# Mamba and local attention, one core: sums over states and the skip term as accumulating DMAs into device memory, in place of pair sums and identity matmuls

## What is computed

```python
dt = softplus(dt_lr @ dt_proj_w.T + dt_proj_b)
dA = exp(einsum('bld,dn->bldn', dt, -exp(A_log)))
dBx = einsum('bld,bln->bldn', dt * x_conv, B_ssm)
h = a_t * h + bx_t                      # scan over tokens
y_t = einsum('bdn,bn->bd', h, c_t)      # sum over 16 states
y = ys + x_conv * D_param               # skip term
out = (y * silu(z)) @ out_proj_w.T
```

## Time and profile before

| what | us |
|---|---|
| median of three runs | 2499.3 |
| profiled execution, its own time | 2501.03 |
| its span, first to last instruction | 2499.2 |
| VectorE (DVE) busy | 2325.9 (93%) |
| TensorE (PE) busy | 2211.9 (89%) |
| ScalarE (ACT) busy | 1336.3 (53%) |
| GpSimd (POOL) busy | 1094.6 (44%) |
| mean granted TensorE clock | 0.957 of full speed |
| DMA | 225.89 MB, mean 90 GB/s |

### The profile page before, as it was taken

How to read it: one execution, slowest core, us unless ns; L and a number is a source line. 1 busy time by engine, 2 the same in 40 slices (tenths; PEclk the granted TensorE clock), 3 DMA queues, 4 the chain that set the end, 5 groups by cost and what they waited for, 6 DMA issues and landing times. The chain is left out here.

```text
span 2499.2 us, 36377 instructions
## 1 busy us (share of the span) xinstructions
PE 2211.9 (89%) x11008; PEld 1363.6 (55%) x11008; DVE 2325.9 (93%) x3159; ACT 1336.3 (53%) x2816; POOL 1094.6 (44%) x973
## 2 busy tenths in 40 slices
PE   4699889998899989989898998989889898899888
PEld 1365555555555555555564655555455555555556
DVE  5999999999999989999899999999999999999984
ACT  3455554555455654546546555465554555555442
POOL 3534355354343553534534436443464425553540
PEclk8899999999999999999999999999999999999999
DMA  3222222222232123222222222322222222222220
GB/s 131 86 91 87 99 81 103 102 73 105 70 124 82 67 102 113 84 97 81 96 87 99 81 95 87 106 85 72 97 101 100 91 74 93 88 98 84 101 85 15
DMA packets 70512, 225.89 MB, mean 90 GB/s; under 512 B 7648, under 2 KB 36640, under 8 KB 51632
## 3 DMA queue, kind: packets, MB, share of 16 engines
q1 hardware_dynamic: 70320, 223.57, 24.8%
HBM read 214.63 MB, written 4.72 MB: 88 GB/s over the span
## 5 line engine op out<-in xcount | busy, mean ns | idle before, releaser
L604 DVE TENSOR_TENSOR_SCAN hb<-dA,state,hb 128x512 f32<-128x512 f32 x512 | 688.5, 1345 | 13.8 <-ACT dA L853 5.6
L1014 POOL COPY state<-hb 128x2 f32<-128x2 f32 x256 | 220.0, 862 | 919.8 <-DVE hb L604 919.8
L1267 PE MATMUL ring<-hT,w 128*128 128x256 f32 (+1 forms) x1536 | 378.4, 405 | 26.7 <-ACT hT L956 26.7
L853 ACT ACTIVATE dA<-dt_sb,amat 128x512 f32<-128x512 f32 x512 | 345.1, 717 | 101.7 <-PE ysum L1131 66.6
L597 DVE TENSOR_TENSOR hb<-u_sb,bc 128x1024 f32<-128x1024 f32 x256 | 350.6, 1370 | 19.9 <-POOL state L1014 19.9
L1267 PEld LDWEIGHTS ring<-hT,w 128*128 128x128 f32 (+1 forms) x1536 | 288.0, 192 | 122.1 <-ACT hT L956 33.8
L611 DVE TENSOR_TENSOR dA<-hb,bc 128x1024 f32<-128x1024 f32 x256 | 327.3, 1279 | 0.0
L935 ACT ACTIVATE probs<-ring,nmax 128x256 f32<-128x256 f32 x512 | 235.3, 476 | 142.3 <-DVE nmax L726 142.2
L1131 PE MATMUL ysum<-dA,ident 128*128 128x512 f32 x512 | 264.1, 611 | 2.8 <-DVE dA L618 2.7
L1060 POOL TENSOR_TENSOR rnorm<-rnorm,powers 128x8 f32<-128x8 f32 x128 | 248.2, 1939 | 23.7 <-POOL rnorm L1057 21.2
L618 DVE TENSOR_TENSOR dA<-dA 128x512 f32<-128x512 f32 x256 | 222.4, 869 | 0.0
(11 more groups left out here) (109 smaller groups left out, 3569.0 us busy)
## 6 DMA issues: line engine op xcount, KB each, us to landing
bc<-bc_rows SPq DMA_DIRECT2D x128, 1024.0 KB, 4.7
wqkv<-in_wqkv SPq DMA_DIRECT2D x48, 512.0 KB, 6.1
w<-in_w SPq DMA_DIRECT2D x16, 1364.0 KB, 8.3
w<-in_w SPq DMA_DIRECT2D x16, 768.0 KB, 5.2
tab<-in_tab SPq DMA_DIRECT2D x64, 128.0 KB, 4.5
xtok<-in_x SPq DMA_DIRECT2D x16, 256.0 KB, 2.9
xres<-in_x SPq DMA_DIRECT2D x16, 256.0 KB, 5.3
out_y<-X SPq DMA_DIRECT2D x16, 256.0 KB, 3.4
```

The lines of the kernel that those rows point to most:

```text
L604: dve.tensor_tensor_scan(hb[:, k % H_RING, :], dA[:, k % DA_RING, :], hb[:, k % H_RING, :], state[:, k:k + 1], ALU.mult, ALU.add).then_inc ...
L853: act.activation(dA[:, k % DA_RING, :], dt_sb[:, j, :], ACT.Exp, scale=amat[:, n:n + 1]).then_inc(dA_ready.sem, 1)
L1014: pool.tensor_copy(state[:, 2 * m:2 * m + 2], hb[:, slot:slot + 2, T - 1]).then_inc(state_saved.sem, 1)
L1267: m = pe.matmul(bank(it, ("h", f, i))[0:rows, part * 256:(part + 1) * 256], w1[:, ft, col:col + rows], hT[:, ft, :], start=(ft == 0), stop ...
```

## The change

The sum of the pairs, the sum over groups and the skip term leave VectorE, TensorE and PSUM. For each pair, GpSimd issues one DMA of both hC tiles (128 partitions x 1024 elements, 512 KB) to a buffer `ysum[j]` in device memory: the first of a half overwrites, the seven others of the tile add to it there (`accum_op=ALU.add`). ScalarE scales xconv by D in place (stage `skip`), and GpSimd adds it with another DMA of 256 KB. At the end of a half GpSimd adds the second 512 columns of `ysum[j]` to the first (stage `merge`, device memory to device memory), SP loads the result into a new tile `y_sb` (stage `y`), and the gate reads that in place of PSUM. Every adding DMA waits, in GpSimd's queue, for the landing of the one before it on the same j. A dA tile is free when the DMA of its pair has landed. The ring of PSUM banks grows from five to seven. The weights `wo` are kept for one layer and loaded per layer (stage `wol`, 512 KB). All five orders are written anew. The scratch of GpSimd's DMAs doubles.

```diff
-BANKS = 5
+BANKS = 7
+ADDS = STATES // GROUP + 2
...
-    diag = sb("diag", [P, NJ, P])
-    ybank = [ctx.enter_context(nc.psum_tensor(f"ysum{j}", [P, T], f32)) for j in range(JH)]
+    ysum = nc.dram_tensor("ysum", [NJ, P, GROUP * T], f32, kind="Internal").ap()
+    y_sb = sb("y_sb", [P, JH, T])
...
+            def load_y(half):
+                for jj in range(JH):
+                    j = half * JH + jj
+                    sp.wait_ge(*added[j].at(it, D16 * ADDS))
+                    sp.wait_ge(*gated.at(it, (half - 1) * JH + jj + 1))
+                    sp.dma_start(y_sb[:, jj, :], ysum[j, :, 0:T]).then_inc(y_loaded[j].sem, D16)
...
-                    dve.wait_ge(*summed.at(it, (half + 1) * SUMS // HALVES - JH + jj + 1))
-                    dve.tensor_tensor(sz[:, j, :], ybank[jj][:, :], sz[:, j, :], ALU.mult)
+                    dve.wait_ge(*y_loaded[j].at(it, D16))
+                    dve.tensor_tensor(sz[:, j, :], y_sb[:, jj, :], sz[:, j, :], ALU.mult)
...
-                if at_ring:
-                    act.wait_ge(*summed.at(it, m + 1))
-                else:
-                    act.wait_ge(*pair_added.at(it, m + 1))
+                if before >= 0:
+                    gb, jb, _ = unit(kb)
+                    act.wait_ge(*added[jb].at(before, adds_after(gb)))
...
+            def add_to_y(m):
+                g, j, _ = unit(2 * m)
+                first = g % (NGROUPS // HALVES) == 0
+                out = 2 * m % DA_RING
+                pool.wait_ge(*hC_ready.at(it, m + 1))
+                if first:
+                    pool.wait_ge(*y_loaded[j].at(it - 1, D16))
+                else:
+                    pool.wait_ge(*added[j].at(it, adds_after(g) - D16))
+                pool.dma_start(ysum[j, :, :], dA[:, out:out + 2, :].rearrange("p n t -> p (n t)"),
+                               accum_op=ALU.bypass if first else ALU.add).then_inc(added[j].sem, D16)
+            def add_skip(half):
+                for j in range(half * JH, half * JH + JH):
+                    pool.wait_ge(*added[j].at(it, D16))
+                    pool.wait_ge(*skip_ready.at(it, j + 1))
+                    pool.dma_start(ysum[j, :, 0:T], xconv[:, j, :], accum_op=ALU.add)
+            def add_halves(half):
+                for j in range(half * JH, half * JH + JH):
+                    pool.wait_ge(*added[j].at(it, D16 * (ADDS - 1)))
+                    pool.dma_start(ysum[j, :, 0:T], ysum[j, :, T:2 * T], accum_op=ALU.add)
...
+            def load_wo(l):
+                sp.wait_ge(*filled(it if l else it - 1, ("wo", NW - 1 if l else NA - 1)))
+                sp.dma_start(wo[:, :, :], io["wo"][:, l, :, :]).then_inc(wo_loaded.sem, D16)
```

More of the change, by code:

```diff
@@ L82 @@
[L82 to L86, removed]
+o(7,2) o(7,3) wo(7) +heads(0) +s(0,0) +s(0,1) +dt(2) +v(0) +pT(0,0) +q(1) hT(3) +dt(3) h(3,0) h(3,1) h(3,2)
@@ L92 @@
[L92 to L96, removed]
@@ L124 @@
-+scan +q(5) ++tail +turn(q,5) +turn(k,5) +scan +scan +q(6) +scan +scan +scan +stats(2) +turn(q,6) +scan
-+turn(k,6) +scan +q(7) ++q(0) +turn(q,7) +turn(k,7) +scan +scan +carry2 +scan
+add(30) +turn(q,0) scan +turn(k,0) add(31) +q(1) +scan +add(0) stats(3) merge(1) +scan +add(1) +scan
++skip(0) ++halo +scan +scan +add(2) +add(3) +turn(q,1) +q(2) +scan +turn(k,1) +scan +add(4) +add(5)
++turn(q,2) +scan +add(6) +add(7) +turn(k,2) +scan +scan ++norm(0) +add(8) +add(9) +q(3) +stats(0) +scan
++turn(q,3) +turn(k,3) +scan +add(10) +add(11) +add(12) +scan +scan +scan ++norm(1) +q(4) +add(13) +carry
@@ L126 @@
++scan +scan +add(14) +add(15) +turn(q,4) +turn(k,4) +add(16) +scan +add(17) +stats(1) +merge(0) +scan
++skip(1) +scan +scan +q(5) +add(18) +add(19) +turn(q,5) +turn(k,5) +scan +add(20) +add(21) +scan +add(22)
++add(23) +scan +scan +q(6) +turn(q,6) +turn(k,6) +q(7) +scan +add(24) +add(25) +scan +stats(2) +turn(q,7)
++turn(k,7) +scan +scan +add(26) +add(27) +add(28) +scan +add(29) +carry2 ++q(0) ++tail +scan
 """
 SP_ORDER = """
-+bc(1) wo(7) +bc(2) xres(1) +bc(3) +q(1) +w1(0) store(0) ++x(0) store(1) +bc(4) +k(1) +k(2) ++x(1) +bc(5)
@@ L577, in _ @@
         dve.tensor_copy(identb[:, :], ident[:, :]).then_inc(casts_done, 1)
-        for j in range(NJ):
-            dve.tensor_scalar(diag[:, j, :], ident[:, :], par[:, C_DP + j:C_DP + j + 1], None, ALU.mult)\
-               .then_inc(diag_ready, 1)
         dve.wait_ge(casts_done, 3)
@@ L624, in fill @@
                 if at_unit[0] == CHUNKS * UNITS:
-                    for _ in range(3):
+                    for _ in range(2):
                         step()
@@ L1100, in stages @@
             return {"halo": load_halo, "norm": rstd_of_x, "tail": save_halo, "q": scale_tables,
-                    "turn": scale_heads, "stats": rstd_of, "scan": keep_state, "carry": carry_xn,
+                    "turn": scale_heads, "stats": rstd_of, "scan": keep_state, "add": add_to_y, "skip": add_skip, "merge": add_halves, "carry": carry_xn,
                     "carry2": carry_x2}
```

178 lines of the change are left out of this document (92 added, 86 removed).

## The result

The kernel became slower: 2533.8 us (median of four runs, 2530.3 to 2539.0) against 2499.5 measured beside it on the same chip, a ratio of 1.014 [1.012, 1.016]. The forecast was 2350, and the range ended at 2480.

What follows compares the result with a forecast made beforehand. VectorE's own work, busy 93% of the span, was taken to set the pace. 2501 - 175 - 25 + 20 + 10 + 15 + 5 = 2351, said as 2350 us; range 2270 to 2480.

Steps and rivals of the forecast that it cites:

- Pair sums off VectorE: VectorE's 256 pair sums leave: 148 us saved if all waiting inside them moves over, 200 if none; with small parts -175.
- Matmuls off TensorE and banks: 297 us off TensorE worth nothing by itself; with two further banks VectorE's waits shorten, bounds 0 and -60, taken -25.
- DMAs on GpSimd: 320 issues at 1 us in GpSimd's queue, covered except ahead of state copies: +20, bounds 0 and +130.
- dA tiles held by a DMA: A dA tile is free only when its add lands, taken 5 us: +10 on today's 5.6 us wait, bounds 0 and +50.
- Load on the DMA engines: DMA share rises from 25% to about 45, at most 65%; shifted rows land later, 32 waits by 0.5 us: +15.
- Scaling on ScalarE: 32 more passes at 0.6 us, 19 us on an engine idle for 47% of the span: zero.
- The way of y: Last add, merge, SP's load and second gate, about 10 us behind some 15 us of VectorE work: +5, bounds 0 and +40.
- Everything hidden: Rival: all waiting goes along with the pair sums and the new order finds 25 us: 2275; 12%.
- GpSimd's queue: Rival: at 2.5 us per issue GpSimd becomes the second bound, 128 us lost at state copies: 2460; 15%.
- Issues and VectorE lock each other out: Rival: each issue holds VectorE's next instruction, 0.5 us giving 2510, 0.2 us giving 2415; 13%.
- Adding DMAs saturate: Rival: over 6.5 us of all sixteen engines per add makes DMA the bound; at 8 us 2930; 13%.
- I would be wrong outright if VectorE waited mostly for something that has no line today: Sign of outright failure: VectorE waiting mostly for something without a line in the earlier waits, y or the B and C rows.

Runs made afterwards that it cites:

- late k weights: Kernel after, with SP loading the next chunk's k weights right after q(7) instead of behind wo(6): 2461.8 us, 72 us less than the kernel after.
- 256 small adds: Kernel before, its own sum untouched, with 256 adding DMAs of 64 KB issued by GpSimd beside it to buffers nobody reads: 2534.8 us.
- plain writes: Kernel before with 256 DMAs of 512 KB writing beside it: 2543.4 us. Kernel after, sum's DMAs writing instead of adding: 2452.1 us, with k weights loaded earlier 2402.0.
- full adds: Kernel before, its own sum untouched, with 256 adding DMAs of 512 KB issued by GpSimd beside it to buffers nobody reads: 2599.6 us.
- the late load alone: Kernel before with only SP's order changed, the next chunk's k weights and two table loads moved behind the shift: 2524.3 us, +24 us.
- six-bank kernel: Kernel after with the k weights loaded earlier and six instead of seven PSUM banks in the ring: 2588.7 us, 127 us more than with seven.
- the small adds: Kernel after with k weights loaded earlier and the seven later adds of each half and tile cut to 128 of 1024 columns: 2395.2 us.

## Why the prediction was wrong, step by step

Two terms of the sum failed, the pair sums (-175, measured -78) and the load on the DMA engines (+15, measured +56 to +67), and one cause had no term at all, the late k weights (+72). The effects measured in separate kernels make this account, and they need not add up exactly: pair sums -78, 256 small adds +35, from small adds to plain writes +9, from these to the full adds +56, late k weights +72. From 2499.5 that gives 2593.5; the kernel after took 2533.8. The rest, -60, is everything that these kernels don't single out: the new order with its banks, the skip term and the merges, the way of y, and what the effects do to each other (the late load alone costs 24, 50 or 72 us, by its surroundings). With plain writes and the early load it comes out alike: 2500 - 78 + 35 + 9 = 2466 against 2402.0, -64.

*Pair sums off VectorE, -175: failed, measured -78.* The busy time came out at the forecast's 2151 us both without the pair sums and in the kernel after (2151.2). That it fits to the microsecond is luck, since 174 was the middle of 148 and 200. What failed is "VectorE's own work sets the pace, and what leaves it shortens the pass as long as no other wait takes its place": other waits took the place of 97 us at once. The small lines of the earlier trace rows were read as what is left to gain; they were the edge of waits that VectorE's work covered. The argument from inside the instructions held: without the pair sums dBx's mean rose from 1370 to 1417 ns and hC's from 1279 to 1308, 20 us of the 25 (200 - 175) that moved over. In the kernel after other instructions took it: dBx fell to 1323, scans went from 1345 to 1367 and hC to 1347.

*Matmuls off TensorE and banks, -25: the first half right, the second of another kind.* "By itself that is worth nothing" held in two kernels. TensorE's busy time came to 2031.8, not 1915: the 576 records of the sums and the skip term are gone, but the durations of the others add up to 2146.1 us instead of 2068.8, 77 more, and they overlap by 40 us less than all did before. The granted clock fell from 0.957 to 0.904 beside it; that it is the cause of the 77 was not shown. The banks' value was argued from the waits of before. The six-bank kernel shows instead that it lies in what the new order can be; some share of the -60 may be theirs.

*DMAs on GpSimd, 1 us each and +20: size right, place wrong.* An issue takes 0.92 us, and GpSimd is busy 1380.4 us of the 1415 forecast. But 256 small adds cost +35 in the old order without dBx waiting any longer for the state copy, and 256 plain writes +43. The wait named (about 40 us) does not exist in the kernel after. What shows in the old kernel with the 64 KB adds is gelu's wait (33.5 instead of 22.6) and dA's (13.4 instead of 5.6). That the DMA an add or a skip term waits for is "long landed" was wrong as well: GpSimd waits 43.2 us for landings ahead of adds, 40.2 ahead of the skip term and 8.8 ahead of the merges.

*dA tiles held by a DMA, +10: right as far as VectorE's own wait shows.* The landing is 7.8 us, not 5, and ScalarE waits 182 us for it, but VectorE waits for the exp 6.6 us in all, against 5.6 before. What those 182 us cost the other work in ScalarE's queue was not measured.

*Load on the DMA engines, +15: failed, +65 to +67 from small adds to full ones, +56 to +60 from writes to adds.* The share (32.6% and 27.5%, 60 together) lies nearer to the 65% of the doubled load than to the 45. By bytes alone 840 us had been worked out for the adds and the reads behind them, and the queue shows 0.326 x 2534.7 = 826; the same bytes written plainly take 0.157 x 2445.6 = 384. That is 5.5 against 2.5 us per MB, a factor of 2.15, and the Trainium skill (Collectives: The Full Stack, The bandwidth ceiling: the fold count and why AG ≠ RS ≠ AR), which puts a summing transfer at half the rate, agrees with this trace in the main; in the old kernel, where all but two of the 256 DMAs add, the factor is 0.315 x 2596.0 = 818 us against 0.132 x 2539.7 = 335, 2.44, and so rather more than the page's. But "hardly changes the sum" was wrong. From the old kernel to the one with writes and the one with adds beside it, the weights land in 6.1, 7.0 and 7.3 us, the shift's last row in 4.6, 5.4 and 6.4, B and C in 4.7, 4.8 and 5.3. (In the kernel after B and C land in 6.3 us, but with plain writes still in 6.1, so most of that is not the adding.) The forecast's 32 waits by 0.5 us was a guess at one of several transfers, and too small even for that one: in the old kernel with adds the landing rose by 1.8 us, and the wait for the shifted rows by 58 us (45.2 to 103.3), as much as 32 times 1.8. With the writes it rose by 15, where 32 times 0.8 would be 26. VectorE already waited in 32 places there, so much or all of each further microsecond was paid; the landing of the other 127 rows is not in the trace.

*Scaling on ScalarE, 0: right in its worth, low in its size.* ScalarE's busy time rose by 61.8 us instead of 19. The scaling passes are 21.2 us. Most of the rest are table loads: ahead of exp and of gelu ScalarE often loads its function table anew, and does so more often in the new order, 61 + 61 loads of 1.28 us instead of 46 + 39, 47 us. They lie on an engine with idle time; what they delay was not measured.

*The way of y, +5: right for the gate.* The gate waits for nothing (no idle time before L821). SP's queue waits 99.6 us for the merges to land ahead of its loads of y, and what that costs the loads behind was not measured. The gate itself takes 0.93 us on average, not 0.67: 8 us over 32, spread.

*What had no step: the late k weights, +72.* The prediction counted SP's added DMAs and priced bc(2) behind y(1), but did not go through the queue for stages that had changed places. The new order was on view, with `+k(7)` behind `+wo(6)`, and what follows `+k(7)` on TensorE needs its load.

The rivals. *Everything hidden*, 2275, is far below what even the small adds or the plain writes with the mended load reach (2395 and 2402). *GpSimd's queue* did not decide; its wait is gone. *Issues and VectorE lock each other out* asked for scans, dBx and hC each longer by 0.1 us; hC is longer by 0.07 and scans by 0.02, dBx is shorter, and VectorE's busy time is the forecast's. What the Trainium skill says there of GpSimd's descriptors (SBUF — State Buffer, SBUF: two separate sides) no run here singles out; by its length, 0.92 us, the issue stayed below the 1 us taken. *Adding DMAs saturate* is the one that ended on the right side, but not by its mechanism: the engines are busy 60% of the span, and an add takes 826 us / 288, 2.9 us of all sixteen, far below its 6.5. "I would be wrong outright if VectorE waited mostly for something that has no line today" came near: 131 of 384 us of idle time are for the square, which had 1.0 us before, and not for B and C (25.1) or y (none).

## What to carry to other kernels

In a kernel whose engines follow orders written out by hand, busy time taken from the bound engine is not time saved: leaving that work out alone, in the old order, gave 45% of it here, and that costs one run. Where a change rewrites the order of a queue, go through it for every load that moved behind a stage that waits, and ask who wants it next; one such load cost 72 us here, where the change with that load mended gains 38. An accumulating DMA took its engines more than twice the time of a write here, and much of what that cost showed in waits for the landings of other transfers, also of one that moves a single row.

## What the runs showed of the hardware

- An issue of a DMA of 128 rows holds GpSimd for 0.58 us when it writes and 0.92 us when it adds (256 issues of each, 147.8 and 221.0 us). Beside the kernel before it is 0.58 and 0.89 us, and an add of 64 KB takes 0.89 as well: the length goes by the kind and not by the bytes.
- Adding 512 KB to device memory lands in 5.5 us beside the kernel before and 7.8 us in the kernel after. A write of the same size lands in 3.4 and 5.3 us. The time of the sixteen engines is 2.44 times that of the writes beside the kernel before, and 2.15 in the kernel after, where an eighth of the DMAs of pairs are writes. A 64 KB add lands in 2.8 us and takes 0.72 us of the sixteen engines (7.3% of 2532.5 us for 256), a 512 KB add 3.2.
- The issue of the shift's second DMA (L529; L503 before) holds SP's queue for 1.5 us in the middle and up to 5.6 (before: 1.4 and up to 7.7), where a B and C load takes 0.33. Beside the 256 adds it is 2.3 us in the middle and up to 9.6, beside the writes 2.0, beside the 64 KB adds 1.5. Whatever load stands behind it starts that much later.
- Loading ScalarE's function table takes 1.28 us each time (ahead of exp and gelu 122 loads after, 85 before; 155 and 118 in all).
- TensorE's mean granted clock was lower where it had less to do: 0.957 before, 0.904 in the kernel after, 0.921 without the sums' matmuls. Constant matmuls put in (512, with six banks) went with 0.93 instead of 0.908 and did not shorten the kernel.
